# A twelve-layer attention program on one core: quantised codes written as smallest steps of fp16, maxima scaled on the vector engine, and no barrier behind the first loads

## The reference

```python
def _fq(x, delta, zp, n_bits):
    xi = _round_ste(x / delta) + zp
    xq = jnp.clip(xi, 0.0, 2.0 ** n_bits - 1.0)
    return (xq - zp) * delta

sim = einsum('bhid,bhjd->bhij', _fq(q, dq, 128.0, 8), _fq(k, dk, 128.0, 8)) * SCALE
attn = softmax(sim, axis=-1)
out = einsum('bhij,bhjd->bhid', _fq(attn, dw, 0.0, 8), _fq(v, dv, 128.0, 8))
```

## Time and profile before

| what | value |
|---|---|
| three runs | 1579.89, 1578.14, 1579.74 us (median 1579.74) |
| the profiled execution's own time | 1576.92 us |
| its span (first to last instruction) | 1575.1 us |
| start up to the first scores of unit 0 | 0 to 33.1 us |
| QSELF, 128 steps | 686 to 997 us |
| QCROSS, 64 steps | 997 to 1159 us |
| mean granted TensorE clock | 0.826 |

### The profile page before, as it was taken

One profiled execution on the slowest core, in us unless ns is written; L12 is line 12 of the kernel. 1 busy time (PEld: TensorE's weight loads), 2 busy tenths in 40 slices (PEclk: granted clock), 3 DMA queues, 4 the chain that ended last, 5 costly groups with the idle time before them and its releaser, 6 DMA issues.

```text
span 1575.1 us, 28607 instructions
## 1 busy us (share of the span) xinstructions
PE 1092.8 (69%) x9344; PEld 593.3 (38%) x9344; DVE 1098.1 (70%) x3102; ACT 894.2 (57%) x2546; POOL 681.1 (43%) x1055
## 2 busy tenths in 40 slices
PE   2888888887788797855353545444358778888888
PEld 1333344444333286831120212222225435453545
DVE  2687777777688653678888999877765666666522
ACT  1555554555554464567676797988852344646531
POOL 3321011011011416558888888877741344445310
PEclk9899999999999998975555555555569799999989
DMA  5213142101331112267555576665530121201000
GB/s 184 61 53 92 51 129 75 54 24 50 99 106 49 42 39 82 57 160 122 99 104 109 106 130 115 121 109 106 109 57 14 27 48 35 49 21 43 1 0 27
DMA packets 265219, 116.53 MB, mean 74 GB/s; under 512 B 216936, under 2 KB 253936, under 8 KB 262896
## 3 DMA queue, kind: packets, MB, share of 16 engines
q1 hardware_dynamic: 260112, 108.29, 30.8%
q0 software_dynamic: 2048, 4.20, 0.9%
q10 hardware_dynamic: 2912, 2.22, 0.5%
HBM read 38.80 MB, written 16.45 MB: 35 GB/s over the span
## 4 chain that ended last, share of the span: by engine, by line
PE 35%; POOL 21%; DVE 18%; issue 14%; ACT 9%; DMA 1%; SPq 0%; POOLq 0%; another core or an unknown queue 0%; ACTq 0%; DVEq 0%
POOL arena L2289 12%; ACT arena L1581 4%; PE acc L1199 3%; POOL inv_total L2278 2%; PE trans L1171 2%; DVE minus_top L1980 2%; PE misc L1021 2%; PE misc L1027 2%; PE trans L1323 2%; ACT arena L1528 2%; PE score L1335 2%; PE score L1337 2%; PE trans L1177 1%; POOL arena L2235 1%; PE acc L1385 1%
## 5 line engine op out<-in xcount | busy, mean ns | idle before, releaser
L2289 POOL TENSOR_SCALAR arena<-arena,inv_total 128x512 f16<-128x512 f32 (+1 forms) x512 | 299.7, 585 | 57.3 <-DVE inv_total L2058 16.8
L1980 DVE TENSOR_REDUCE minus_top<-score 128x4 f32<-128x616 f32 (+4 forms) x256 | 200.6, 802 | 95.3 <-PE score L1141 36.9
L2154 POOL TENSOR_TENSOR rstd<-spread,minus_half 128x4 f32<-128x4 f32 x36 | 37.5, 1043 | 489.5 <-DVE spread L1662 414.0
L1581 ACT ACTIVATE arena<-score,minus_top,exp_scale 128x512 f32<-128x512 f32 (+1 forms) x340 | 210.4, 625 | 20.9 <-POOL arena L2289 11.9
L1528 ACT ACTIVATE arena<-trans 128x512 f32<-128x512 f32 x240 | 134.4, 596 | 109.3 <-PE trans L1177 104.0
L1619 ACT ACTIVATE arena<-arena,minus_top 128x154 f32<-128x154 f32 x256 | 105.2, 412 | 129.3 <-DVE minus_top L2123 129.1
L1280 PE MATMUL score<-arena 32*128 32x512 bf16 (+1 forms) x340 | 68.9, 458 | 139.7 <-ACT arena L1581 138.7
L2064 DVE TENSOR_REDUCE top_score<-score 128x2 f32<-128x1024 f32 (+1 forms) x128 | 135.7, 1061 | 0.6 <-PE score L1280 0.5
L2309 POOL TENSOR_TENSOR arena<-arena,inv_total 128x512 f32<-128x512 f32 x64 | 66.5, 1040 | 143.9 <-DVE inv_total L2131 130.0
L1581 ACT ACTIVATE arena<-trans,minus_top,exp_scale 128x154 f32<-128x154 f32 (+1 forms) x172 | 105.5, 620 | 19.2 <-POOL arena L2289 14.9
L2118 DVE CUSTOM_DVE_ANT_0 arena<-score,arena 128x154 f32<-128x154 f32 x256 | 65.9, 313 | 60.6 <-PE score L1360 60.2
(11 more groups left out here) (283 smaller groups left out, 2814.4 us busy)
## 6 DMA issues: line engine op xcount, KB each, us to landing
arena<-q_terms SPq DMA_DIRECT2D x88, 128.0 KB, 2.8
late<-arena SPq DMA_DIRECT2D x128, 64.0 KB, 2.0
q_terms<-arena SPq DMA_DIRECT2D x36, 128.0 KB
late<-k_terms SPq DMA_DIRECT2D x32, 128.0 KB, 3.1
arena<-arena SPq DMA_TRANSPOSE x192, 3.1
by_expert<-zeros SPq DMA_DIRECT2D x2, 1472.0 KB, 9.8
arena<-by_expert SPq DMA_DIRECT2D x10, 256.0 KB
from_expert<-arena SPq DMA_DIRECT2D x10, 256.0 KB
```

The source lines that it names most:

```text
L1581: ins = nc.scalar.activation(probs[:, i % 3, j, of], quant_score[i % 3][:, j, of], ACT.Exp, bias=minus_top[:, at_col:at_col + 1], scale=ex ...
L1980: nc.vector.tensor_reduce(dst, src, axis=AX.X, op=ALU.max, negate=True).then_inc(top_ready, 1)
L2289: ins = nc.gpsimd.tensor_scalar(codes[:, (i - 1) % CODE_SOURCES, j, to], probs[:, (i - 1) % 3, j, of], inv_total[:, at_col:at_col + 1], HA ...
```

## The change

1. The codes are written as smallest steps. `CODE_STEP` is 2^-24, the smallest fp16 number above zero. The inverse of the sum carries that factor, POOL's instruction becomes a product and a bound (multiply, then minimum with 255 steps) and its output is rounded to a whole number of steps by the conversion to fp16. PE reads these fp16 numbers as they are; the values' codes are fp16 too, and the factor 2^24 is put into the scale of the output. The copy on DVE (L2047) goes; PE waits for the DMA transposes themselves.
2. The maxima are scaled by a DVE tensor_scalar behind the reduce, in its own wait for the reduce; ACT's instruction L1572 goes.
3. The block `once` and its barrier go. Its instructions stand at the head of each engine's stream in the one block, and single waits take the barrier's place (`ident_in`, `first_weights_in`, `pads_in`, `pool_set`, `dve_set`). The first weights are issued second on SP; the eight late loads are issued behind the reads of the queries of unit 0; ACT runs one copy early (`first_use`), behind which its function table is loaded. Four of the first eight query reads move from SP to ACT. POOL's additions to x of sequences 0 and 1, which need a late load, move one place back, behind the padding rows of sequence 1.

```diff
-HALF_ROUND = 1024.0
+CODE_STEP = 2.0 ** -24
...
-                at(exact, f + 1, ("x", nxt), ("pads", nxt))
+                at(exact, f + 1, ("x", nxt), ("pads", nxt), ("base", 0), ("base", 1))
...
-        v_quant, v_quant_tail = put([P, 2, TILES, HEADS, 32], bf16), put([P, 2, HEADS, 32], bf16)
+        v_quant, v_quant_tail = put([P, 2, TILES, HEADS, 32], fp16), put([P, 2, HEADS, 32], fp16)
...
-        pT_codes = put([P, CODE_SLOTS, 2 * TILES, P], bf16)
-        put = place(arena, [pT_at])
-        pT_raised = put([P, CODE_SLOTS, 2 * TILES, P], fp16)
+        pT_codes = put([P, CODE_SLOTS, 2 * TILES, P], fp16)
...
             @block.sync
             def _(sp):
+                sp.dma_start(ident[:, :], io["ident"]).then_inc(ident_in, 16)
+                sp.dma_start(attn_w[:, 0:4, :], io["attn_w"][:, 0:4, :]).then_inc(first_weights_in, 16)
                 for dst, src in loads:
                     sp.dma_start(dst, src).then_inc(weights_in, 16)
...
-                        read_queries(slice(0, 2), q_first)
+                        read_queries(slice(0, 2), q_first, slice(0, PRODUCTS // 2))
                     read_queries(slice(0 if u else 2, PAIRS), q_stacked)
                     if u == 0:
+
+                        for dst, src in late_loads:
+                            sp.dma_start(dst, src).then_inc(late_in, 16)
...
-                    pe.wait_ge(codes_copied, 2 * n + 2)
+                    for i in (2 * n, 2 * n + 1):
+                        pe.wait_ge(codes_turned[i % CODE_SLOTS], 16 * (i // CODE_SLOTS + 1))
...
+                act.wait_ge(first_use_set, 1)
+                nc.scalar.copy(first_use[:, 1:2], first_use[:, 0:1])
...
+                act.wait_ge(q_out, 48)
+                for n in range(PRODUCTS // 2, PRODUCTS):
+                    act.dma_start(q_stack[n::PRODUCTS, 0, 0:2, :], scratch["q"].ap()[:, Q_TERMS[n], 0:2, :]).then_inc(q_first, 16)
+                act.wait_ge(dve_set, DVE_SETS)
...
                     act.wait_ge(quant_top, i + 1)
-                    nc.scalar.activation(of_step(minus_top, i), of_step(top_score, i), ACT.Copy,
-                                         scale=exp_scale[:, of:of + 1]).then_inc(quant_top_scaled, 1)
                     if i >= 3:
                         act.wait_ge(codes_ready, i - 2)
-                    act.wait_ge(quant_top_scaled, i + 1)
...
-                def copy_codes(i):
-
-                    of = i % CODE_SLOTS
-                    dve.wait_ge(codes_turned[of], 16 * (i // CODE_SLOTS + 1))
-                    nc.vector.tensor_scalar(pT_codes[:, of, :, :].rearrange("p k q -> p (k q)"),
-                                            pT_raised[:, of, :, :].rearrange("p k q -> p (k q)"),
-                                            -HALF_ROUND, 255.0, ALU.add, ALU.min).then_inc(codes_copied, 1)
...
-                        nc.vector.tensor_reduce(of_step(top_score, i), src, axis=AX.X, op=ALU.max,
-                                                negate=True).then_inc(quant_top, 1)
-                    if QUANT_LAG <= i < quant_steps + QUANT_LAG:
-                        copy_codes(i - QUANT_LAG)
+                        then(nc.vector.tensor_reduce(of_step(top_score, i), src, axis=AX.X, op=ALU.max, negate=True))
+                        of = stage(QUANT_STEPS[i][0]) - QSELF
+                        nc.vector.tensor_scalar(of_step(minus_top, i), of_step(top_score, i), exp_scale[:, of:of + 1], None,
+                                                ALU.mult).then_inc(quant_top, 1)
...
-                                                         inv_sizes[:, 3:4], None, ALU.mult))
+                                                         inv_sizes[:, 3:4], CODE_STEP, ALU.mult, ALU.mult))
...
-                                                              inv_total[:, at_col:at_col + 1], HALF_ROUND, ALU.mult, ALU.add)
+                                                              inv_total[:, at_col:at_col + 1], 255.0 * CODE_STEP, ALU.mult, ALU.min)
```

More of the change, by code:

```diff
@@ L614, in build @@
         cleared = sem("cleared")
+        first_use_set = sem("first_use_set")
+        pool_set = sem("pool_set")
+        dve_set = sem("dve_set")
         v_cols_cleared = sem("v_cols_cleared")
@@ new lines, in build @@
+        FIRST_SEQUENCE_LOADS, PAD_LOADS, REST_LOADS = 2, 2, 2
+        loads = [(sizes[:, :], io["sizes"].partition_broadcast(P)), (cols[:, :], io["cols"]),
+                 (term_row[:, :], io["term_row"])]
+        late_loads = [(rows[:, :, :], io["rows"].partition_broadcast(P)), (norm_sel, io["norm_sel"]),
+                      (attn_w[:, 4:20, :], io["attn_w"][:, 4:20, :]), (expert_no[:, :], io["expert_no"]), (masks_f, io["masks"]),
+                      (ffb_cols[:, :], io["ffb_cols"]),
+                      (router_w[:, :], io["L1_xattn_router_w"]),
+                      (router_b[:, :], io["router_b"].partition_broadcast(P))]
@@ L794, in build @@
+        LATE_LOADS = len(late_loads)
+        POOL_SETS, DVE_SETS = 12, 27
         with nc.Block() as block:
@@ L797, in _ @@
             def _(sp):
+                sp.dma_start(ident[:, :], io["ident"]).then_inc(ident_in, 16)
+                sp.dma_start(attn_w[:, 0:4, :], io["attn_w"][:, 0:4, :]).then_inc(first_weights_in, 16)
+                for dst, src in loads:
+                    sp.dma_start(dst, src).then_inc(weights_in, 16)
                 for u in EXACT_UNITS:
@@ L985, in item @@
                         if is_cross(u):
+                            if u == 0:
+                                pe.wait_ge(first_weights_in, 16)
                             pe.wait_ge(misc_read, out_of("ctx", b))
@@ L1994, in split_tops @@
                     nc.vector.tensor_tensor(to[:, :, :, :, 2], left, to[:, :, :, :, 1], ALU.subtract).then_inc(top_split, 1)
+                dve.wait_ge(cleared, 4)
+                for j in range(4):
+                    at_row = 32 * top_place(j)
+                    nc.vector.memset(ones[at_row:at_row + 3, j, :], 1.0).then_inc(dve_set, 1)
+                    nc.vector.memset(ones_tail[at_row:at_row + 3, 32 * j:32 * j + CTX_TAIL], 1.0).then_inc(dve_set, 1)
+                for s in range(2):
+                    nc.vector.memset(ones_pad[s * STACK:s * STACK + 3, :], 1.0).then_inc(dve_set, 1)
+                for j in range(4):
+                    rows_j = slice(32 * j, 32 * j + CTX_TAIL)
+                    for i in range(2):
+                        at_col = i * (P + HD) + 32 * j + 16
+                        nc.vector.memset(v_tail[rows_j, :, at_col:at_col + HD], 1.0).then_inc(dve_set, 1)
+                nc.vector.memset(minus_half[:, :], -0.5).then_inc(dve_set, 1)
+                dve.wait_ge(ident_in, 16)
+                dve.wait_ge(weights_in, 16 * len(loads))
+                nc.vector.tensor_copy(ident_bf[:, :], ident[:, :]).then_inc(dve_set, 1)
+                nc.vector.reciprocal(inv_sizes[:, :], sizes[:, :]).then_inc(dve_set, 1)
+                for n, name in enumerate(["L1_xattn_sa_bq", "L1_xattn_ca_bq"]):
+                    nc.vector.tensor_scalar(q_bias[:, n:n + 1], col(name), float(HD) ** -0.5, None, ALU.mult).then_inc(dve_set, 1)
+                for n in range(2):
+                    q, k, vv, w = (sizes[:, 4 * n + i:4 * n + i + 1] for i in range(4))
+                    nc.vector.tensor_scalar(exp_scale[:, n:n + 1], q, k, float(HD) ** -0.5, ALU.mult, ALU.mult).then_inc(dve_set, 1)
+                    nc.vector.tensor_scalar(out_scale[:, n:n + 1], vv, w, 1.0 / CODE_STEP, ALU.mult, ALU.mult).then_inc(dve_set, 1)
+                dve.wait_ge(dve_set, DVE_SETS)
+                dve.wait_ge(pool_set, POOL_SETS)
                 for it in BEFORE[0]:
@@ L2056, in _ @@
                         if is_cross(QUANT_STEPS[i - 2][0]):
-                            then(nc.vector.tensor_scalar(t, t, sizes[:, 7:8], None, ALU.mult))
+                            then(nc.vector.tensor_scalar(t, t, sizes[:, 7:8], 1.0 / CODE_STEP, ALU.mult, ALU.mult))
                         nc.vector.reciprocal(v_, t).then_inc(quant_inv, 1)
@@ L2161, in item @@
                     b = seq(u)
-                    if name == "x":
+                    if name == "x" and u > 1 or name == "base":
                         pool.wait_ge(misc_raised, out_of("x", u))
```

130 lines of the change are left out of this document (47 added, 83 removed).

## The result

| | before | changed |
|---|---|---|
| median of the runs compared | 1578.94 us (4 runs) | 1913.87 us (4 runs, 1903.49 to 1917.63) |
| ratio | | 1.2131, interval 1.2096 to 1.2166 |
| span of the profiled execution | 1575.1 us | 1913.6 us |
| first scores of unit 0 | 33.1 us | 25.0 us |
| QSELF, from its first maxima to those of QCROSS | 685.7 to 996.6: 310.9 | 682.8 to 1274.3: 591.5 |

A forecast was written before the change was run, and what follows sets the result against it. No engine bounds a whole stage: ACT and POOL level in plain self steps, DVE with items, ACT in plain cross steps. Terms 7.5 + 12 + 10 + 0.5 = 30 us off the 1579.74 median gave 1550, range 1527 to 1569.

The forecast's parts named there:

- The rest: Last codes reach PE without the copy: 0.5 us less; fp16, POOL's minimum and the factors in the scales cost nothing.
- The start, 7.5: Kernel start: no barrier, earlier loads and query reads split with ACT make it 7.5 us shorter, bounds 4 and 9.
- QSELF, 12: Quantised self stage: copies and ACT scalings out, DVE scalings in; 12 us less, 10 where DVE bounds, 2 elsewhere.
- QCROSS, 10: Quantised cross stage: ACT's step loses its scaling, POOL then bounds; 10 us less, bounds 4 and 24.
- 0.13 a step: Quantised self stage: net gain in us taken for some 80 steps where DVE is the bound, 10 us.
- rival D: Self steps: exponentials wait for DVE's scaling, which waits for POOL's codes; 19 us more there, total 1591; chance 6%.
- Rival B: Quantised stages: buffers swallow the items, POOL busy from end to end in self; 54.5 us less, total 1525; chance 20%.

The follow-up runs named there:

- a1_add_zero: The changed kernel with multiply, add 0.0 in place of multiply, minimum in POOL's codes instruction, without the bound to 255: 1543.64 us, 0.9773 of before.
- b_start_alone: The kernel before with only the third part of the change (no barrier, loads and reads moved): 0.9973 of before (0.9943 to 1.0003).

## Why the prediction was wrong, point by point

The forecast was 1550, range 1527 to 1569, faster at 0.89. Measured 1914.

**The step that failed** stands under "The rest": "POOL's minimum in place of an addition ... change no shape; I cost them at nothing." It is the whole error: the forecast was missed by 364 us, and with this operator alone put back 370 go. I had seen the risk in the next sentence but put it on the numbers, not on the operator, and gave it no chance: "were they slower, each 10% would be 18 us in QSELF". It came out 177% slower (1995 against 721 ns), so by that very scale 318 us in QSELF, where 294 were measured (591.5 against 297.7 with the addition); POOL, one of two level engines, took the stage over. A duration was carried from one row to an instruction that shared its engine, shape and types and differed in its second operator. No row of the kernel before had POOL's tensor_scalar with a minimum, so the price should have been an unknown with an open upper end, and a rival of its own.

With that one operator put back (a1_add_zero, 1543.64, on a chip where before took 1580.79), the sum of the other terms can be read. That it lands inside the range is in part luck: the start was sized too high, QCROSS too low, and QSELF's term is near only as the net of two parts that were not priced apart.

- **The start, 7.5.** In the changed kernel PE began at 5.68 (forecast 5.3), DVE masked the keys at 9.62 (9.6), the first scores came at 24.97 (25.5), 8.1 earlier than before:

```profile
5.68 0.45 PE L904 MATMUL misc<-ident,arena 128*128 128x128 f32 x1 [5.68 <-DMA x<-in_x]
...
9.62 0.32 DVE L1683 TENSOR_TENSOR arena<-misc,arena 128x154 f32<-128x154 f32 x1 [0.76 <-PE misc L937]
...
20.54 7.75 SPq L756 DMA_DIRECT2D arena<-q_terms  x12
20.54 2.40 ACTq L1479 DMA_DIRECT2D arena<-q_terms  x4
...
24.97 0.31 PE L1078 MATMUL score<-arena 64*128 64x154 bf16 x2 [12.67 <-DMA arena<-q_terms]
```

  The chain was right at each point, the term as a gain of the whole was not: about 4 remain at the end (b_start_alone), and at the beginning of QSELF 2.3 in that run's profile and 2.9 in the changed kernel's. I followed the lead to the first scores and no further.
- **QSELF, 12.** Measured 13.1 (310.86 to 297.74), but of two terms that I had as one: the copy, with POOL's shorter inverse, gave 23.5, the scaling took 10.4 back. The product took 487 ns on average, twice the 240 of L2057 that I took as nearest; that this wait would often take the copy's place was said, and 0.13 a step was near enough to the net only.
- **QCROSS, 10.** Measured 18.6 (166.0 to 147.4), inside the bounds of 4 and 24. The term was about half of it. By DVE's maxima a step without items fell from 2.24 to 1.86, where I had 1.94, and the steps with items from 3.03, 2.88, 4.18 and 3.40 to 2.87, 2.79, 4.18 and 3.10. I had taken POOL for the bound of a plain step, and so took 5 us back for the item that it carries. A window of nearly five plain steps in a1_add_zero, and POOL's codes of one step in its timeline, say otherwise:

```profile
1025.00:1034.00 9.00, 4.88 (x51) 1.82 (x51) 7.09 (x20) 9.00 (x41) 7.55 (x20) 0.50 0.85 150
```

```profile
1024.90 1.53 POOL L2294 TENSOR_SCALAR arena<-arena,inv_total 128x154 f16<-128x154 f32 x4 [0.33 <-DVE inv_total L2041]
```

  ACT is busy for all of the 9.00 us, POOL for 7.55: its four codes take 1.53 of a step of 1.86 and it waits 0.33 for DVE. ACT is the bound, and POOL's item lay hidden beside it; the 5 us were wrongly taken back.
- **The lock behind the maxima, rival D.** Its mechanism is real (ACT waits 76.6 us for the scaling in a1_add_zero) and costs 10 us in QSELF; but D had that stage 19 longer than before on balance, and it is 13 shorter. D was 6%, the only rival that named a slower kernel, and it is not what made this one slower: in the changed kernel the scalings take 229 ns by their median. That one of the two engines waits for a whole instruction of the other, as I read from the copy at 927.42, agrees with the trace where the codes are fast: in a1_add_zero the 85 scalings that began 0.03 to 0.48 us into a codes instruction all ended 0.02 to 0.03 behind it. Where they are slow it does not: 94 of 128 scalings ran whole inside one of POOL's instructions of 1992 ns.
- **Rival B.** It would have shown itself by POOL idle for less than 12 us before its inverse in QSELF; in a1_add_zero POOL waits 41.9 there for DVE. That POOL is busy from end to end in the changed kernel has another cause, the operator.
- **The rest.** PE reads the small fp16 numbers as it read bf16 (307 ns a matmul before and in the changed kernel); writing them costs POOL nothing (692 ns median before, 696 in a1_add_zero).

## What to carry to other kernels

An instruction's price held here for its operators too, not for engine, shape and type alone: on POOL's tensor_scalar a pair of multiply and add took 692 ns for 512 elements, and every other form tried took 1.5 to 2.9 times as long at its size, a plain multiply included. When a change swaps an operator on an engine that is level with the bound, measure that one instruction first, with an open upper end in the range until then. And a narrow product put behind a reduce on DVE does not stay short if POOL's wide instructions hold it up (487 ns on average where 228 is the least): put the wait where nobody is waiting, stage by stage.

## What the runs showed of the hardware that I had not expected

- POOL's tensor_scalar, fp32 in and fp16 out: multiply-add at 692 to 696 ns for 512 elements and 400 for 154, multiply-multiply at 692 for 512, add-multiply at 398 for 154; multiply-minimum, multiply-maximum, minimum-multiply and multiply-subtract at 1992 to 1997 for 512; a single multiply at 677 for 154, slower than multiply and add 0 together (403).
- POOL writes (696 ns against 692), the DMA transpose carries (3.1 us from issue to landing before and in a1_add_zero) and PE reads (307 and 306 ns a matmul) fp16 numbers down to 2^-24 at no cost in time.
- The slow codes do not keep DVE out from end to end. In the changed kernel's QSELF the 84 scalings that began 0.50 to 1.17 us into a codes instruction of 2 us took 0.23 each; the 10 that began in its first 0.33 ended 0.70 to 0.71 into it, and of those that began 1.39 to 1.78 into it, 20 in all, each ended 0.02 to 0.03 behind it.
